# Recurrent layer plus quantised linear layer on eight cores: the skip term moved to VectorE for all banks, and the tile's order of work changed

## What is computed

```
xn = layernorm(x)                                   # over the 2048 columns
# branch s, a small recurrent layer and a low-rank layer
a  = layernorm(xn) * gamma + beta
u  = a @ W_in + b_in                                # 8 numbers a row
h  = scan(u): h[t] = sigmoid(decay) * h[t-1] + u[t] # along the sequence
r  = xn + h @ W_out + b_out + a * D_skip            # the residual
s  = r + relu(layernorm'(r) @ W_down + b_down) @ W_up + b_up   # 32 hidden units
# branch g, a linear layer on fake-quantised 8-bit values
y  = relu(quant8(xn) @ quant8(kernel) + quant8(bias))          # 2048 x 2048
g  = silu(quant8(y))
out = x + s * g
```

## Time and profile before

| | |
|---|---|
| median of 3 runs | 621.19 us (620.35 to 621.38) |
| profiled execution | 621.07 us |
| its span, first to last instruction, slowest core | 619.5 us |
| spans of the 8 cores | 616.3 to 619.5 us |
| TensorE matmul busy | 562.0 us, 91% |
| VectorE busy | 515.0 us, 83% |
| ScalarE busy | 522.9 us, 84% |
| GpSimd busy | 441.8 us, 71% |

### The profile page before, as it was taken

The page is one execution under the profiler, slowest core; times in us unless marked ns, Lnnn a source line. Parts: engine busy times, 40 slices in busy tenths (PEclk is TensorE's granted clock), DMA queues, the critical chain, the costliest instruction groups (busy, mean ns, idle before and its releaser), DMA issues.

```text
span 619.5 us, 10127 instructions; the slowest of 8 cores (616.3 to 619.5 us)
## 1 busy us (share of the span) xinstructions
PE 562.0 (91%) x3570; PEld 277.3 (45%) x3570; DVE 515.0 (83%) x1182; ACT 522.9 (84%) x500; POOL 441.8 (71%) x708
## 2 busy tenths in 40 slices
PE   0458776999999999999999999999999999999993
PEld 0455553344444444444444444444444444444441
DVE  3899937698888888888888888888888899888855
ACT  2858868699999999899999999999999999999974
POOL 2568653578877777777777888777777777877740
PEclk9768779799999999999999999999999999999998
DMA  8998720477777776787776777666887677676423
GB/s 242 339 334 238 258 68 1 102 196 188 196 200 196 196 196 201 203 195 201 194 206 187 208 195 180 189 193 197 205 204 203 188 187 188 188 204 197 128 85 135
DMA packets 137523, 117.84 MB, mean 190 GB/s; under 512 B 126208, under 2 KB 126208, under 8 KB 127360
## 3 DMA queue, kind: packets, MB, share of 16 engines
q1 hardware_dynamic: 137472, 117.19, 68.2%
HBM read 52.17 MB, written 33.55 MB: 138 GB/s over the span
## 4 chain that ended last, share of the span: by engine, by line
PE 81%; DVE 7%; DMA 5%; ACT 3%; POOL 2%; SPq 1%; issue 1%; POOLq 0%; DVEq 0%
PE py L517 69%; PE pu L568 3%; PE px L644 3%; DMA g<-L_ffn_kernelT 3%; DMA x<-L_ffn_kernelT 2%; PE px L576 2%; DVE kst L333 2%; PE px L606 1%; PE pt L635 1%; DVE st L482 1%; ACT k L350 1%; PE pt L590 1%; ACT zT L387 1%; PE pu L603 1%; SPq L691 1%
## 5 line engine op out<-in xcount | busy, mean ns | idle before, releaser
L517 PE MATMUL py<-kq,ixT 128*128 128x512 bf16 x2048 | 466.3, 382 | 0.5 <-ACT py L502 0.5
L517 PEld LDWEIGHTS py<-kq,ixT 128*128 128x128 bf16 x2048 | 195.4, 98 | 227.4 <-issue 13.3
L656 POOL TENSOR_TENSOR x<-x,g 128x512 f32<-128x512 f32 x124 | 155.1, 1272 | 60.1 <-DVE g L651 57.7
L613 ACT ACTIVATE junk<-px 128x2048 bf16<-128x2048 f32 x32 | 60.1, 1878 | 50.7 <-PE px L606 50.7
L502 ACT ACTIVATE py<-brow,st 128x512 f32<-128x512 f32 x128 | 86.9, 679 | 3.5 <-DVE st L525 2.3
L525 DVE CUSTOM_DVE_ANT_0 t<-py,sc_bc,st 128x512 f32<-128x512 f32 x96 | 71.5, 745 | 21.9 <-PE py L517 21.7
L442 DVE BATCH_NORM_STATS2 t<-x 128x6 f32<-128x512 f32 x128 | 81.4, 680 | 2.3 <-DMA x<-L_attn_x 2.3
L651 DVE TENSOR_TENSOR g<-px,g 128x512 f32<-128x512 f32 x124 | 77.0, 683 | 3.2 <-PE px L644 3.2
L482 DVE TENSOR_REDUCE st<-xc 128x1 f32<-128x2048 f32 x32 | 72.8, 2276 | 0.9 <-ACT xc L475 0.9
L466 POOL TENSOR_SCALAR zix<-xc,ln 128x2048 bf16<-128x2048 f32 x32 | 65.5, 2045 | 3.7
L491 ACT ACTIVATE zix<-xc,c,st 128x2048 f16<-128x2048 f32 x32 | 66.6, 2082 | 0.0
(11 more groups left out here) (162 smaller groups left out, 623.2 us busy)
## 6 DMA issues: line engine op xcount, KB each, us to landing
x<-L_attn_x SPq DMA_DIRECT2D x32, 1024.0 KB, 5.3
out<-x SPq DMA_DIRECT2D x31, 1024.0 KB, 4.1
x<-L_ffn_kernelT SPq DMA_DIRECT2D x7, 1024.0 KB, 14.7
g<-L_ffn_kernelT SPq DMA_DIRECT2D x3, 1024.0 KB, 16.4
t<-L_ffn_kernelT SPq DMA_DIRECT2D x2, 1024.0 KB, 15.8
xc<-L_ffn_kernelT SPq DMA_DIRECT2D x2, 1024.0 KB, 16.6
spare<-L_ffn_kernelT SPq DMA_DIRECT2D x2, 1024.0 KB, 16.9
out<-x SPq DMA_DIRECT2D x4, 256.0 KB, 2.0
```

The lines of the kernel that those rows point to most:

```text
L517: P.put(lambda e, j=j: e.matmul(bank[:], ixT[c % 2][:, 128 * j:128 * (j + 1)], kq[:, D * j + 512 * q:D * j + 512 * (q + 1)], start=False, ...
L656: G.put(lambda e: e.tensor_tensor(x_t[c % 4][:, 512 * q:512 * (q + 1)], x_t[c % 4][:, 512 * q:512 * (q + 1)], g_t[:, 512 * q:512 * (q + 1) ...
```

## The change

`NB` goes: all four banks get their skip term from `v_skip`, and all four seeds come from the row tile `gdr`, now 2048 wide (it takes the whole of `spare`). `p_skip` and `diag` are removed. Two small operations of `v_amax` go to GpSimd (`g_scales`). The two scans are separate steps. In the loop, `p_out` stands inside q3 behind its fourth matmul, `v_hidden` and `p_hfT` stand in the next pass, and `p_up` behind the second matmul of q1. In the start, tile 1's z and whole numbers are turned by DMA, no longer by TensorE (units "z1" and "i1"), and tile 1 has an order of its own in pass 1. Cut to its core:

```diff
-NB = 2
-        gdr = spare[:, 0:NB * 1024].bitcast(F32)
-        diag = spare[:, NB * 1024:NB * 1024 + (4 - NB) * 512]
+        gdr = spare[:].bitcast(F32)
...
-        turns = ["k0", ..., "k13", "z1", "k14", "i1", "k15"]
+        turns = ["k0", ..., "k13", "k14", "k15"]
...
         def turn_z(c):
             Y.dma(...,
-                  d_z[c % 2], f"z{c}", f"p1_{c - 2}" if c >= 2 else None, mark=f"zT{c}")
+                  d_z[c % 2], f"z{c}", f"pu{c - 2}" if c >= 2 else "wup2", mark=f"zT{c}")
...
         def v_amax(c):
...
-            V.put(lambda e: e.tensor_scalar(st[:, 6:7], st[:, 3:4], ln[:, 1:2], 1.0 / 127.0, OP.mult, OP.mult), f"ln{c}")
-            V.put(lambda e: e.tensor_scalar(st[:, 5:6], st[:, 4:5], ln[:, 7:8], None, OP.mult), f"inv{c}",
+        def g_scales(c):
+            st, ln = cell(c)
+            G.put(lambda e: e.tensor_tensor(st[:, 5:6], st[:, 4:5], ln[:, 7:8], OP.mult), f"inv{c}",
                   f"pb{c - 3}_3" if c >= 3 else None, mark=f"inv0_{c}")
+            G.put(lambda e: e.tensor_scalar(st[:, 6:7], st[:, 3:4], ln[:, 1:2], 1.0 / 127.0, OP.mult, OP.mult),
+                  f"ym{c - 3}" if c >= 3 else None, mark=f"ys{c}")
...
         def s_seed(c):
-                if q < NB:
-                    S.put(... gdr ..., bias=ln[:, 6:7], scale=1.0)
-                else:
-                    S.put(... xc_t[c % 2] ..., bias=0.0, scale=ln[:, 1:2])
+                S.put(... gdr ..., bias=ln[:, 6:7], scale=1.0)
         def v_skip(c):
-            for q in range(NB):
+            for q in range(4):
-        def p_skip(c):
...
         # start
-        for n in range(2, 13):
+        for n in range(2, 12):
             load_k(n)
-        load_x(1)
         (loads of the small weights)
-        for n in range(13, 16):
+        for n in range(12, 16):
             load_k(n)
-        load_x(2)
-        load_x(3)
+        for c in range(1, 4):
+            load_x(c)
...
+            if i == 1:
+                (tile 1's own order: v_evac(0, 3), v_ymax, s_gate, p_half(1, 0, 0), p_low(1), p_half(1, 0, 1), v_hidden(0),
+                 p_hfT(0), v_low(1), v_evac(1, 0), v_hfa(0), s_bias(1, 2), s_center(2), p_half(1, 1, 0), p_up(0), p_uT(1),
+                 g_z(2), turn_z(2), v_gated(0), g_add(0, 0..3), v_amax(2), g_scales(2), s_seed(1), s_quant_x(2), g_ixb(2))
+            else:
+                v_evac(i - 1, 3)
+                v_ymax(i - 1)
+                v_hidden(i - 1)
+                s_gate(i - 1)
+                p_half(i, 0, 0)
+                p_hfT(i - 1)
+                v_amax(i + 1)
+                g_scales(i + 1)
+                s_quant_x(i + 1)
+                v_hfa(i - 1)
+                p_low(i)
+                p_half(i, 0, 1)
+                p_part(i, 1, 0, 2)
+                p_up(i - 1)
+                s_bias(i, 2)
+                v_low(i)
+                v_evac(i, 0)
+                v_gated(i - 1)
+                g_add(i - 1, 0)
+                g_ixb(i + 1)
+                g_add(i - 1, 1..3)
+                s_seed(i)
+                p_part(i, 1, 2, 8)
+                p_uT(i)
+                store(i - 1)
             p_half(i, 1, 1)
+            v_scan(i, 0)
             v_evac(i, 1)
-            v_scan(i)
             v_skip(i)
+            v_scan(i, 1)
             p_half(i, 2, 0)
             p_half(i, 2, 1)
-            p_skip(i)
+            p_part(i, 3, 0, 4)
             p_out(i)
+            p_part(i, 3, 4, 16)
             s_bias(i, 3)
             s_square(i)
             (statistics, projection, evac q2, biases, centring, norm, z: as before)
-            p_half(i, 3, 0)
-            v_hidden(i)
-            p_half(i, 3, 1)
-            p_hfT(i)
```

More of the change, by code:

```diff
@@ L512, in p_half, with p_part @@
         def p_half(c, q, half):
+            p_part(c, q, 8 * half, 8 * half + 8)
+        def p_part(c, q, j0, j1):
             bank = py[q % 2]
-            turned = (f"C_k{4 * q + 3}_0", f"C_k{4 * q + 3}_1") if c == 0 and half == 0 else ()
-            lies = f"C_i{c}_1" if c < 2 else f"ixT{c}"
-            for j in range(8 * half, 8 * half + 8):
+            turned = (f"C_k{4 * q + 3}_0", f"C_k{4 * q + 3}_1") if c == 0 and j0 == 0 else ()
+            lies = f"C_i{c}_1" if c < 1 else f"ixT{c}"
+            for j in range(j0, j1):
                 P.put(lambda e, j=j: e.matmul(
@@ L732, in build_nc @@
         v_amax(0)
+        g_scales(0)
         step(2)
@@ L768, in build_nc @@
         step(12, 12)
+        step(13, 13)
+        k_rows(2)
+        step(14, 14)
+        s_rows(2)
+        v_evac(0, 0)
+        s_bias(0, 2)
+        step(15, 15)
+        g_piece("wout")
+        g_piece("wup")
+        p_gdrow(0)
+        s_gdrow(0)
+        p_wg()
         v_stats(1, 0)
@@ L812, in build_nc @@
         s_seed(0)
+        s_quant_x(1)
+        g_ixb(1)
+        v_evac(0, 2)
         s_bias(1, 0)
-        p_skip(0)
-        v_evac(0, 2)
-        v_scan(0)
+        v_scan(0, 0)
         v_skip(0)
+        v_scan(0, 1)
         p_half(0, 3, 1)
         p_out(0)
+        v_proj(0)
+        s_square(0)
+        g_rstd2(0)
         v_stats(2, 0)
@@ L851, in build_nc @@
                 v_hidden(0)
                 p_hfT(0)
+                v_low(1)
+                v_evac(1, 0)
                 v_hfa(0)
-            if m:
+                s_bias(1, 2)
+                s_center(2)
+                p_half(1, 1, 0)
+                p_up(0)
+                p_uT(1)
+                g_z(2)
+                turn_z(2)
+                v_gated(0)
+                for q in range(4):
+                    g_add(0, q)
+                v_amax(2)
+                g_scales(2)
@@ L855, in build_nc @@
                 v_low(i)
                 v_evac(i, 0)
-            if not m:
-                last(i - 1)
-                continue
-            v_gated(i - 1)
-            g_add(i - 1, 0)
-            if a:
-                g_ixb(i + 1)
-            for q in range(1, 4):
-                g_add(i - 1, q)
-            if m:
+                v_gated(i - 1)
+                g_add(i - 1, 0)
+                if a:
+                    g_ixb(i + 1)
+                for q in range(1, 4):
+                    g_add(i - 1, q)
```

160 lines of the change are left out of this document (61 added, 99 removed).

## The result

The changed kernel takes **640.13 us** (median of 4 runs, 639.90 to 640.99) against 621.11 for the kernel before on the same chip (4 runs, 620.35 to 621.38): a ratio of 1.031, interval 1.0293 to 1.0329. It is slower by 3.1%. The forecast was 637.3 in a range of 627 to 646, slower with a chance of 0.85. The profiled execution took 639.9 us, its span is 638.4.

What follows compares the result with a forecast made beforehand. TensorE was taken to pace the kernel before at 16.14 us a tile, and a VectorE-ScalarE ring the changed one at 16.91. 621.07 + 21.6 (loop) - 4.5 (start) - 0.9 (end) = 637.3 us, range 627 to 646.

Steps and rivals of the forecast that it cites:

- The loop term: Loop: each tile grows by 0.77 us over 28 intervals of 16.14, +21.6 us.
- Ring two: Loop, closed chain of VectorE and ScalarE through evac q2, gate and gated products: 15.61 grows to 16.91 us; chance 0.80.
- Ring one: Loop, closed chain of ScalarE and TensorE from square through q2 and p_out to next square: 16.14 grows to 16.42 us.
- The start: Before the loop: the first gate of the loop comes 4.5 us earlier, ends -9 and +2.
- the 3.89 and 1.94 on ScalarE: Start: ScalarE's idle time for wup2 and two evictions go, bringing tile 0's q3 units forward by at most 5.8 us.
- now hidden stands ahead, worth some 3.6: Start, tile 1: TensorE's 4.37 us wait for v_hidden, queued behind amax, shrinks, worth some 3.6 us.
- ixT1 comes late: Start: tile 1's input, quantised after the seeds, converted, then transposed by DMA, becomes the limit, so gains do not add.
- The end: Last two tiles: -1.4 us with TensorE leading, +0.5 for a later up-projection; sum -0.9, ends -1.5 and +0.5.
- rival C: Loop: with two gaps a tile TensorE's clock falls to 0.84, stream 18.3 us a tile, total about 675 us; chance 0.03.
- A: Loop: TensorE goes on setting the pace at 15.59 us a tile, total 600 us; chance 0.08.
- B: Loop: the chain over p_out leads at 16.42 us a tile, VectorE's staying below, total 623.5 us; chance 0.09.
- VectorE idle over 1 us before the gated products: Loop, sign of being right: VectorE waits over 1 us there, released by ScalarE's gate.

Runs made afterwards that it cites:

- e1: Changed kernel with the skip products of banks 2 and 3 left out of every tile; 630.16 us, ratio 1.015.
- e6: Kernel before with four skip products on VectorE and none on TensorE, all orders as before; 647.9 us, ratio 1.0438.
- e9: Loop of the kernel before behind the changed kernel's start, with tile 1's quantisation, tile 0's evac q3 and ymax, tile 2's centring moved earlier; 613.62 us, ratio 0.9886.
- e10: Changed kernel with the skip products of banks 2 and 3 left out and p_out straight behind q2; 606.86 us, ratio 0.9768.
- e7: Changed kernel with the first two statistics of tile i+2 moved on VectorE behind the hidden units, ahead of amax; 806.47 us, ratio 1.2994.
- e3: Changed kernel with evac q2 ahead of the statistics and the second scan behind the mean on VectorE; 638.11 us, ratio 1.0279.
- e4: Changed kernel with the gate's silu in two halves, so gated products start after the first; 638.63 us, ratio 1.0295.

## Why the prediction was right

**The loop term** (+21.6 forecast, right). 28 x (16.89 - 16.14) = 21.0. Ring two was to be 16.91 and is 16.89, every stage within 0.03. Ring one was to be 16.42 and measured 16.52 in e1: `p_out` comes 4.43 after q2, not 4.32, the one stage that I had put together from single matmuls rather than read. e6 shows the cause alone: two more skip products in the old order, the same tile.

**The start** (-4.5 forecast, -1.3 measured; inside its ends of -9 and +2). This is the term that was mis-sized. TensorE's three waits in the start of the changed kernel, the issue of the transfer that the first of them is for, and the loop's first gate:

```profile
93.92 2.04 SPq L490 DMA_TRANSPOSE ixT<-zix  x1
...
98.39 3.57 PE L514 MATMUL py<-kq,ixT 128*128 128x512 bf16 x8 [4.33 <-ACT py L496]
...
115.45 1.04 PE L514 MATMUL py<-kq,ixT 128*128 128x512 bf16 x4 [2.56 <-ACT py L496]
...
122.68 1.89 PE L514 MATMUL py<-kq,ixT 128*128 128x512 bf16 x8 [3.16 <-DMA ixT<-zix]
...
122.85 1.99 ACT L537 ACTIVATE q<-t,st 128x2048 uint8<-128x2048 f32 x1
```

The first square comes at 94.10 instead of 99.75: 5.65, nearly the 5.8 that the step "the 3.89 and 1.94 on ScalarE" gives as the most. Then the step "now hidden stands ahead, worth some 3.6" failed: from the first square to the second it takes 22.79 us, more than the 21.0 of the earlier trace rows. The wait for `v_hidden` is gone, but three others stand there: 4.33 us for tile 1's input, quantised at 89.81 behind the seeds (98.39; the row names a bias, but the bias that this matmul needs was written at 91.80, and the transposing DMA was issued at 93.92, 4.47 before the matmul; tile 2's, which the third row names, is issued at 118.23, 4.45 before its matmul), 2.56 for a bias of q3 (115.45), and 3.16 for tile 2's transposing DMA (122.68). The forecast had named the first of these ("ixT1 comes late") without giving it a size, and had not seen the other two. The first gate is at 122.85 (forecast near 121; before, 125.8) and the interval behind it is 18.5, where the loop's are 16.9: -2.9 + 1.6 = -1.3. e9 shows what was there to be had: with the three mends together, and with the skip of two banks on TensorE, the first gate is at 114.2. How much each of the three waits is worth by itself was not separated.

**The end** (-0.9 forecast, -0.7 measured). The last two intervals of the gate are 15.73 and 15.69 (before 16.22 and 16.07): -0.9 where the forecast had -1.4; and from the last gate to the end it takes 9.54 us instead of 9.36: +0.2 where it had +0.5. The two misses offset each other, which is luck. Sum: 21.0 - 1.3 - 0.7 = 19.0, and the two spans differ by 18.9.

**Two slips in the sums.** The upper corner of the range is 621.1 + 28 + 2 + 0.5 = 651.6, not 649, and rival C's stream is 15.59 / 0.84 = 18.6 a tile, so about 683 us, not 675. Neither touches the forecast.

**The rivals.** A, TensorE sets the pace: in the form stated it falls, since e10 reaches a full TensorE at 15.70 only with both extra products out. The Trainium skill, Perfetto Trace Analysis, section Identifying the Most-Contended Engine, names the engine with the highest occupancy as the one to optimize first, and adds that TensorE's headroom is to be judged by MFU (the matmul work done as a share of the peak) and by the share of weight loads. The prediction applied it by matmul busy time, and so applied, the trace here does not bear it out: TensorE was full, 0.55 us a tile was taken off it and put on VectorE as 1.30, and the tile grew by 0.75. By weight loads TensorE was busy 7.54 of 16.14 us, less than VectorE with 14.22. B, ring one at 16.42: the ring exists (e1), but is hidden under ring two. C, the clock falls: not here, the loop's clock is 1.00. In e7, where TensorE waits some 4 us in a tile of 22, the loop's clock is 0.88, so the mechanism exists in this kernel but not in the changed loop. The Trainium skill, TensorE: Matmul & The Clock Gate, Part 1, ties the clock to how busy the engine has recently been; both rows agree with that.

**The signs.** All but one stood as named: "VectorE idle over 1 us before the gated products" did not. The idle time is 1.5 (forecast about 1.4), but 0.76 of it stands there and 0.78 before amax, for centring, a wait that the forecast had not placed. VectorE is busy 15.15 (15.3 forecast) and the first gate is at 122.85 (near 121).

## What to carry to other kernels

Before work moves from a full engine to one with time to spare, list the closed rings that run through both, with their slack. Here VectorE had 1.9 us a tile idle, and its ring 0.53: of 1.30 us moved, 0.75 came out as time. Shortening one ring uncovers the next, here 0.06 us (e3, e4) to 0.37 us (e1) below it, so lay out all of them before predicting a gain, through TensorE too, and in an in-order queue look up when the transfer lands before an operation is moved ahead.

## What the runs showed of the hardware

- TensorE's clock. In the changed loop TensorE waits twice a tile for a bias (at most 1.0 us between weight loads, 0.5 us between matmuls), and the granted clock stayed at 1.00 for 478 us. In e7 waits of about 4 us in tiles of 22 came with a mean of 0.88. Behind such a wait the stream runs at the lower of the two levels, 1.2 GHz: the last two rows of e7's timeline are weight loads, 0.43 us apart, each for one matmul over 512 columns, and in the loop of before such matmuls came 0.213 apart.
- A small operation that needs the result of its neighbour on VectorE started later than one that does not. In e3 the aggregate starts at 305.75, the mean's last step, which needs it, 0.29 later, and the scan, which does not need that step, 0.07 behind it. The aggregate itself stands directly behind the statistics that it needs in e3 and starts 1.32 after the second pair of them (304.43); in the changed kernel evac q2 stands there and starts 1.20 after its pair (305.18, 306.38). That is 0.1 us of what e3 did not gain.
